# A gated cross-attention and feed-forward block: hand-written starts and endings of all engines around a loop of eight periods, other PSUM banks, and the score maxima of a pair of heads in one reduce

## The reference: what is computed

```python
x = x + tanh(g_xattn) * xattn(layernorm(x), ctx, Wq, Wkv_expand, Wout)
x = x + tanh(g_ffn) * ffn(layernorm(x), w_gate, w_up, w_down, up_reorder_index, down_reorder_index)

def xattn(q, latent_kv, Wq, Wkv, Wout):
    qp = q @ Wq.T
    k, v = split(latent_kv @ Wkv.T, 2)
    scores = where(causal, einsum('bhqd,bhkd->bhqk', heads(qp), heads(k)) / sqrt(32), min)
    return merge(einsum('bhqk,bhkd->bhqd', softmax(scores), heads(v))) @ Wout.T

def reorder_quantize(x, idx):
    scale = max(abs(x)) / (448 * 6)
    xr = (x / scale)[:, idx]
    scale_x = max(abs(xr), axis=1) / 448
    return fp8(xr / scale_x), scale_x, scale

def qlinear(qx, scale_x, scale, W, idx, out_idx=None):   # W: rows quantised to fp8 in the same way
    y = (qx * scale_x) @ (qw * w_scale).T * scale
    return y if out_idx is None else y[:, out_idx]

def ffn(x, w_gate, w_up, w_down, up_idx, down_idx):      # 512 -> 1408 -> 512
    qx = reorder_quantize(x, up_idx)
    t = silu(qlinear(*qx, w_gate, up_idx, down_idx)) * qlinear(*qx, w_up, up_idx, down_idx)
    return qlinear(*reorder_quantize(t, down_idx), w_down, down_idx)
```

## Time and profile before

| | |
|---|---|
| median of 3 runs (lowest, highest) | 742.02 us (741.12, 743.23) |
| profiled execution, its own time | 744.06 us |
| profiled execution, its span | 742.3 us |
| mean granted TensorE clock of the span | 0.965 |
| busy: TensorE, VectorE, ScalarE, GpSimd | 663.5, 664.0, 552.3, 551.3 us |
| instructions profiled | 15885 |

### The profile page before, as it was taken

One profiled execution on the slowest core, in us unless ns is written; L12 is line 12 of the kernel. 1 busy time (PEld: TensorE's weight loads), 2 busy tenths in 40 slices (PEclk: granted clock), 3 DMA queues, 4 the chain that ended last, 5 costly groups with the idle time before them and its releaser, 6 DMA issues.

```text
span 742.3 us, 15885 instructions
## 1 busy us (share of the span) xinstructions
PE 663.5 (89%) x6130; PEld 420.9 (57%) x6130; DVE 664.0 (89%) x1193; ACT 552.3 (74%) x987; POOL 551.3 (74%) x606
## 2 busy tenths in 40 slices
PE   2566889899999999999999999999999999888672
PEld 2445666566666666666565656565666666443220
DVE  6997866989999999899999989898989899998983
ACT  4978779796878787878788787879697959384430
POOL 6577897877878787878879787878787876575341
PEclk9858899999999999999999999999999999999996
DMA  8889776768575666685757565765748565130321
GB/s 288 205 193 165 158 161 106 151 147 155 127 133 115 144 122 135 98 173 92 169 89 157 105 153 112 142 129 129 132 122 137 134 100 133 24 100 16 79 67 48
DMA packets 151208, 95.52 MB, mean 129 GB/s; under 512 B 115326, under 2 KB 121854, under 8 KB 151134
## 3 DMA queue, kind: packets, MB, share of 16 engines
q1 hardware_dynamic: 148974, 92.68, 59.9%
q0 software_dynamic: 576, 1.45, 0.6%
q10 hardware_dynamic: 1584, 0.39, 0.2%
HBM read 31.59 MB, written 9.83 MB: 56 GB/s over the span
## 4 chain that ended last, share of the span: by engine, by line
PE 69%; DVE 12%; ACT 8%; issue 4%; DMA 4%; POOL 2%; SPq 0%; ACTq 0%; POOLq 0%; DVEq 0%
PE pair L730 37%; PE pair L957 6%; PE pair L962 5%; PE pair L932 3%; PE pair L987 3%; PE pair L983 3%; PE pair L988 3%; PE pair L931 2%; PE pair L891 2%; DVE mx L1691 2%; PE pair L893 2%; PE pair L892 2%; DMA PT<-in_L_xattn_Wq_dram 1%; DMA Q<-mT 1%; DVE rsum L1695 1%
## 5 line engine op out<-in xcount | busy, mean ns | idle before, releaser
L607 POOL TENSOR_TENSOR room<-room,up_scale 128x512 f32<-128x512 f32 (+1 forms) x96 | 121.9, 1277 | 43.6 <-ACT room L1363 43.2
L591 POOL TENSOR_SCALAR_AFFINE_SELECT PT<-PT 128x512 f32<-128x512 f32 x128 | 88.0, 700 | 41.6 <-ACT PT L1338 40.7
L1338 ACT ACTIVATE PT<-pair 128x768 f32<-128x768 f32 x128 | 99.8, 810 | 12.8 <-PE pair L962 6.4
L1363 ACT ACTIVATE room<-room,sx 128x512 f32<-128x512 f32 (+1 forms) x96 | 64.9, 679 | 47.3 <-DVE room L1762 47.2
L730 PE MATMUL pair<-WdT,room 128*128 128x512 bf16 x352 | 85.3, 393 | 14.8 <-DMA room<-room 9.8
L730 PE MATMUL pair<-WgT,room 128*128 128x512 bf16 (+1 forms) x384 | 91.3, 361 | 7.0 <-DMA room<-room 3.8
L730 PE MATMUL pair<-WuT,room 128*128 128x512 bf16 (+1 forms) x384 | 91.3, 362 | 1.9 <-DVE room L1762 1.7
L730 PE MATMUL pair<-xT,WqTh 128*128 128x256 bf16 x512 | 88.6, 275 | 1.7 <-ACT exact L1150 1.7
L1691 DVE TENSOR_REDUCE mx<-pair 128x2 f32<-128x512 f32 x128 | 87.3, 682 | 0.0
L1368 ACT ACTIVATE room<-room 128x512 bf16<-128x512 f32 (+1 forms) x96 | 54.7, 586 | 39.6 <-DVE room L1779 38.7
L730 PE MATMUL pair<-xT,WqTl 128*128 128x256 bf16 x256 | 70.5, 275 | 0.0
(11 more groups left out here) (137 smaller groups left out, 1902.6 us busy)
## 6 DMA issues: line engine op xcount, KB each, us to landing
xin<-in_x_dram SPq DMA_DIRECT2D x16, 512.0 KB
K<-kh SPq DMA_DIRECT2D x32, 256.0 KB
Q<-qh SPq DMA_DIRECT2D x32, 256.0 KB
x<-in_x_dram SPq DMA_DIRECT2D x16, 512.0 KB, 4.5
out_dram<-x SPq DMA_DIRECT2D x16, 512.0 KB, 3.1
K<-kl SPq DMA_DIRECT2D x16, 256.0 KB
Q<-kl SPq DMA_DIRECT2D x16, 256.0 KB
room<-in_L_ffn_w_down_dram SPq DMA_DIRECT2D x4, 704.0 KB, 7.5
```

The lines of the kernel that those rows point to most:

```text
L591: pool.affine_select(out=view, in_=view, compare_op=ALU.is_ge, fill=0.0, base=0, pattern=[[0, 2], [0, 2], [1, P]], channel_multiplier=-1). ...
L607: pool.tensor_tensor(g, g, up_scale[:, chunk(n)[1]], ALU.mult).then_inc(slw_done, 1)
L1338: act.activation(head_columns(ring(b, c), 0, 384), head_columns(shifted_pair[c][:, :], 0, 384), ACT.Exp, scale=SCALE).then_inc(exp_done, 1)
L1363: act.activation(g, g, ACT.Silu, scale=sx[:, chunk(n)[0]:chunk(n)[0] + 1]).then_inc(silu_done, 1)
```

## The change

It has four parts.

**1. Maxima.** For a pair of heads, the reduces of 256 and of 512 columns become one reduce of 768 columns seen as 2 x 3 x 128, into three columns of `mx` a head, which is widened from TT to TT + 1 columns. A new step, `second_maxima(b)`, joins the last two of them for all 16 heads; `max_parts` waits for it.

```diff
-        mx = sb("mx", [P, NH, TT])
+        mx = sb("mx", [P, NH, TT + 1])
...
-                dve.tensor_reduce(mx[:, heads, 0], head_columns(w, 0, P), AX.X, ALU.max)
-                dve.tensor_reduce(mx[:, heads, 1], head_columns(w, P, 3 * P), AX.X, ALU.max).then_inc(max_done, 1)
+                dve.tensor_reduce(mx[:, heads, :], head_columns(w, 0, 3 * P).rearrange("p h (r s) -> p h r s", s=P), AX.X,
+                                  ALU.max).then_inc(max_done, 1)
+
+            def second_maxima(b):
+                dve.wait_ge(max_done, 8 * b + 8)
+                dve.tensor_tensor(mx[:, :, 1], mx[:, :, 1], mx[:, :, 2], ALU.max).then_inc(max_joined, 1)
```

**2. Order.** The loops with conditions go. Each engine has a list for the beginning, a loop of eight periods, and a list for the ending. SyncE's, cut:

```diff
-            for k in range(-8, NB + -1):
-                if k == -4:
-                    unit_loaded(13)
-                at(k + 5, stack_keys, 0)
-                if k == -7:
-                    load_w_kv()
...
+            unit_loaded(0)
+            unit_loaded(1)
+            load_x(0)
+            load_w_kv()
+            unit_loaded(3)
+            load_c(0)
+            load_w_q()
+            mask_of_queries(1)
+            no_maxima(0)
+            unit_loaded(2)
+            unit_loaded(5)
+            unit_loaded(4)
+            turn_x(0, 0)
+            mask_of_keys(0)
+            load_w_out()
+            turn_x(0, 1)
...
+            for k in range(1, 9):
+                store(k)
+                stack_queries(k + 4, 0)
...
+            turn_qt(14, 1)
+            turn_qt(15, 0)
+            turn_qt(15, 1)
+            store(13)
+            store(14)
+            store(15)
```

**3. Banks.** The PSUM banks of several steps change:

```diff
-        turn_bank = bank[2]
-        weighted_bank = (bank[3], bank[5])
+        turn_bank = bank[3]
+        weighted_bank = (bank[3], bank[4])
...
-        gate_bank = (bank[7], bank[1], bank[0], bank[4], bank[1], bank[3])
+        gate_bank = (bank[7], bank[1], bank[0], bank[1], bank[0], bank[1])
...
-        down_bank = (bank[4], bank[3])
-        aw_bank = (1, 0, 0, 3, 7, 0, 5, 1, 2, 3)
...
+        down_bank = (bank[5], bank[3])
+        aw_bank = (2, 6, 0, 1, 7, 6, 5, 3, 6, 2)
```

**4. Waits.** Waits that the new order implies are left out, or kept only for some batches, as in SyncE's transpose of x:

```diff
             def turn_x(b, t):
-                sp.wait_ge(xl_done, 2 * b + t + 1)
-                if t == 0 and b:
+                if t == 0 and b == 0:
+                    sp.wait_ge(cl_done, 1)
+                if t == 0 and b == 1:
+                    sp.wait_ge(xl_done, 3)
+                if t == 0 and b >= 1:
                     sp.wait_ge(v_made, 2 * b)
...
```

3610 lines of the change are left out of this document (2710 added, 900 removed).

## The result

The changed kernel takes 789.62 us (median of 4 runs, 784.21 to 790.38) against 742.62 (4 runs): a ratio of 1.062, 95% interval 1.057 to 1.066. It is slower by 47 us where 731.5 was forecast. The profiled execution took 784.21 us, the lowest of the four; its span is 782.5 us, 40.2 more than the span of before.

What follows compares the result with a forecast made beforehand. TensorE was taken to bound the middle, VectorE the end. Start 5.5, filling 0, loop 0 and end 5 sum to 10.5 us off the 742.0 median: 731.5 us, forecast 727 to 735, wider range 722 to 742.

Steps and rivals of the forecast that it cites:

- The bound of the middle: From 136 to 637.7 us TensorE works 500.28 of 501.70 us; only work taken from TensorE would shorten it.
- Part 4: The loop over batches: the new order costs 0, bounds -0.3 and +0.5 us a batch over 12 batches.
- (c): VectorE's circle in the loop: waits grow by 0.9 us, join adds 0.25, reduces return 0.5; slack left 0.4 us.
- Rival C: Slower: VectorE's circle in the loop exceeds TensorE's 38.6 us; 747 us at 1.3 us a batch; chance 0.09.
- Part 1: The maxima: merged reduce 946 ns, join 0.25 us; VectorE saves 4 us in all, mostly hidden under TensorE.
- Part 2: The start: keys of batch 0 at 33 us, first scores at 64.6; gain 5.5 us, bounds 0 and 11.
- the last stacking DMA: At the start, ahead of the first scores: takes 7.0 of the 8.9 us from stacking to scores, as before.
- Part 3: Filling of the pipeline, from the first scores until 136 us: 0 us, bounds -3 and +3.
- Part 5: The end: interleaving batches 14 and 15 leaves 2 us of VectorE's 6 us gaps; gain 5, bounds 1 and 8.

## Why the prediction was wrong

**The bound of the middle** was right for the old order (TensorE without gaps) and was taken to be a property of the kernel. It was one of the order.

**Part 4, the loop, is the step that failed.** It said 0, with bounds of -0.3 and +0.5 us a batch; measured were 3.2 (41.90 - 38.72), 3.5 a batch from batch 2 to 14. Two terms failed. First, (c) kept VectorE's durations of the earlier trace rows and added up only waits, with 0.4 us left. But a step's duration belongs to where it stands: five forms got longer by 2.8 us a batch since GpSimd works beside them, as cutting GpSimd's work shows. The walk through the orders looked at each engine's list and its waits, and never laid VectorE's SBUF steps beside GpSimd's. Second, the banks: "all gate chunks but the first now share two banks, with 2 us to spare" was short by 2.6 us, since TensorE waits 0.56 us there. Measured shares: undoing the order takes 2.6 us away, and the 0.6 left is what the banks cost in the old order. In the new order the bank is 0.66 us (undone in the changed kernel), GpSimd's work 1.7 (left out), and 1.1 stays when both are gone; they don't add up exactly (3.2), since cutting GpSimd saves less, 1.4, once the bank is repaired. Two things stay open: the cause of the 1.1, and how much of GpSimd's share is VectorE's longer steps and how much GpSimd's own chain.

**Rival C was the right side**, and its engine, VectorE, is the likeliest one, though no run shows its circle alone to set the period of the new order. Its place (residual 1 and down_scaled 1 behind the later down) was not it, its price of 1.3 us was less than half, and its chance of 0.09 was far too low for a slack of 0.4 us in 38.6 with all orders changed. The point from which it decides (0.9 us a batch) was passed more than threefold.

**Part 1** was right: 946 ns forecast and 949 measured, the join 200 ns for 250, nothing gained while TensorE covers. VectorE's busy time fell by 2.0 us where it said 4.

**Part 2** was right in its first term and wrong in what it was worth. Keys of batch 0 begin at 33.78 (forecast 33); w_out was issued at 24.38 and took 7.1 us (6 were taken), but the wait that ended last was another, for VectorE's rounding of a tile of w_down (TensorE goes on at 31.78), so part of the hit is luck. The first scores come at 66.92 (forecast 64.6, before 70.15), 3.2 us earlier and not 5.5. The term that failed is the last stacking DMA, taken over at 7.0 us:

```profile
55.07 0.59 SPq L419 DMA_DIRECT2D Q<-kl  x1
...
66.92 0.26 PE L1338 MATMUL pair<-K,Q 125*128 125x128 bf16 x1 [5.28 <-issue]
```

It was issued 2.4 us before the 57.5 of the forecast (55.7 + 1.8), and the scores came 11.9 us behind it. The last maxima of batch 0 end at 80.5 us, before 80.2, and its row sums come 3.8 us later. **Part 3** is the term that was mis-sized: 0, with bounds of 3 us, measured some 11 us from the first scores to the sums of batch 2 (3.2 gained turned into 7.7 lost), 7.0 of them by the sums of batch 0. It had nothing on the send of the maxima, which came 4.2 us late behind three loads. The absolute value of a weight tile among the exponentials, which it named, held batch 0 up only in the run in which these loads were moved.

**Part 5** was right in its mechanism: VectorE needs 52.2 us from its last group sums to its last rounding (forecast 54, before 58.7), and idles for 1.8 of them (forecast 2, before 6). That 5.1 us were measured for the ending alone, with 5 forecast, is in part luck, since the ending gained 7.5 and its change-over took 2.7.

## What to carry to other kernels

Before an order is changed, list for each engine not only what it waits for but what runs beside it: here VectorE's elementwise steps on SBUF lasted up to three times as long beside a wide GpSimd step as alone, and a profile's mean holds only for the order in which it was taken. A middle that is bound by one engine "without gaps" may have an engine just below it (here 36.4 us in 38.7); a rise of its busy time, not of its waits, can turn the bound over, as the small reduces did in the old order. Changes that come as one (order, banks, beginning, ending) should be run apart: the ending here was worth 5 us, and nobody could see it under 52 lost elsewhere.

## What the runs showed of the hardware

VectorE's elementwise steps on SBUF took longer beside wide GpSimd steps, at most two and a half to three times as long: flooring of 1408 columns 0.58 us alone and 1.45 beside one, rounding of 512 columns 0.41 and 1.26. A flooring that started during a wide GpSimd step ended 0.4 us behind that step's end, whether it had started 0.21 or 0.65 us into it. Reduces, and steps with an operand in PSUM, did not change; inside a GpSimd step of two columns the flooring took 0.59. GpSimd's steps changed both ways in the middle: its causal cut went from a mean of 702 to 848 ns and its scaling of up (512 columns) from 1276 to 1477, but its scaling of 384 columns from 1224 to 1073 and the low part of the queries from 1393 to 1224; in sum it was busy for 1.0 us a period more.

A DMA on the path took longer behind large loads: 7.3 us for the send of batch 0's maxima and not 3.1, with three loads issued 2 to 3 us ahead of it.
